# Layer 1's gate: root and inverse lengths placed half a step earlier in the order of work

## The reference

```python
qkv = shift_token(x) @ wqkv               # 8 heads of 64
q = l2norm(q) * q_scale                   # t / max(|t|, 1e-12)
k = l2norm(k) * k_scale
q, k = rotary_xpos(q, k)
o = local_attention(q * 8, k, v)          # windows of 64, each sees itself and the one before
x = x + o @ wo
h = layernorm(shift_token(x)) * lg + lb
a, g = split(h @ w1 + b1)
x = x + (a * gelu(g)) @ w2 + b2
```

## Time and profile before

| | us |
|---|---|
| median of 3 runs (5014.09 to 5020.99) | 5015.04 |
| the profiled execution | 5018.97 |
| its span | 5017.2 |
| mean granted clock of PE | 0.948 |
| PE, DVE, ACT, POOL busy in the span | 4451.9, 3169.0, 2488.4, 2285.9 |

### The profile page before, as it was taken

One profiled execution on the slowest core, in us unless ns is written; L12 is line 12 of the kernel. 1 busy time (PEld: TensorE's weight loads), 2 busy tenths in 40 slices (PEclk: granted clock), 3 DMA queues, 4 the chain that ended last, 5 costly groups with the idle time before them and its releaser, 6 DMA issues. The chain is left out here.

```text
span 5017.2 us, 68570 instructions
## 1 busy us (share of the span) xinstructions
PE 4451.9 (89%) x27252; PEld 2196.7 (44%) x27252; DVE 3169.0 (63%) x4190; ACT 2488.4 (50%) x3838; POOL 2285.9 (46%) x1307
## 2 busy tenths in 40 slices
PE   6999999997886788887789999996799999999998
PEld 3444444444564334333322222222455555555554
DVE  4756575736665777773278777865565666666565
ACT  2344444446664466562256666663344444444444
POOL 0455555567773487790100000000166666676674
PEclk8999999998998799898889999997899999999999
DMA  1000000002110000000000000000000000000000
GB/s 33 3 3 3 3 3 3 3 1 59 31 31 19 3 2 1 2 1 24 3 1 1 2 2 1 1 1 16 5 1 3 3 1 3 3 3 1 3 1 9
DMA packets 62001, 36.80 MB, mean 7 GB/s; under 512 B 36356, under 2 KB 53936, under 8 KB 61424
## 3 DMA queue, kind: packets, MB, share of 16 engines
q1 hardware_dynamic: 61680, 32.41, 2.5%
HBM read 22.03 MB, written 1.05 MB: 5 GB/s over the span
## 5 line engine op out<-in xcount | busy, mean ns | idle before, releaser
L799 DVE TENSOR_REDUCE L_part<-banks 128x2 f32<-128x1024 f32 (+2 forms) x1600 | 1880.4, 1188 | 938.7 <-PE banks L650 810.3
L784 ACT ACTIVATE L_weights<-banks 128x1024 f32<-128x1024 f32 (+1 forms) x1600 | 1556.4, 999 | 1063.7 <-PE banks L682 836.3
L708 PE MATMUL banks<-L_weights,L_V 128*32 128x512 f32 (+3 forms) x6400 | 1491.4, 603 | 2.8 <-ACT L_raw L733 1.8
L1035 POOL TENSOR_TENSOR L_wsum<-L_wsum,L_weights 128x1024 f32<-128x1024 f32 (+3 forms) x436 | 962.1, 2207 | 54.1 <-ACT L_weights L784 2.4
L1018 POOL TENSOR_TENSOR L_wsum<-L_wsum,L_two 128x1024 f32<-128x1024 f32 x238 | 568.0, 2386 | 823.3 <-DVE L_two L1000 820.5
L708 PEld LDWEIGHTS banks<-L_weights,L_V 128*64 128x64 f32 (+1 forms) x6400 | 282.7, 123 | 467.8 <-issue 406.0
L2433 POOL MEMSET A3m_ones<- 128x128 f32 x1 | 0.2, 204 | 1060.2 <-POOLq L97 1060.2
L650 PE MATMUL banks<-L_KH,L_QH 64*128 64x512 f32 (+3 forms) x1664 | 399.6, 437 | 45.4 <-DVE L_part L799 27.5
L682 PE MATMUL banks<-L_QH,L_KH 64*128 64x512 f32 (+3 forms) x1664 | 410.3, 428 | 18.1 <-issue 10.2
L682 PE MATMUL banks<-L_QL,L_KH 64*128 64x512 f32 (+3 forms) x1664 | 371.7, 382 | 0.0
L682 PE MATMUL banks<-L_QM,L_onesrow 64*128 64x512 f32 (+3 forms) x1664 | 371.6, 381 | 0.0
(11 more groups left out here) (438 smaller groups left out, 5873.3 us busy)
## 6 DMA issues: line engine op xcount, KB each, us to landing
F_early<-F_V SPq DMA_DIRECT2D x63, 128.0 KB, 2.3
F_tab<-xpos SPq DMA_DIRECT2D x8, 512.0 KB, 4.2
F_h<-L_ffn_h_w SPq DMA_DIRECT2D x2, 1024.0 KB, 8.2
F_wqkv<-L_ffn_wqkv SPq DMA_DIRECT2D x2, 768.0 KB
L_cos<-rope_cos SPq DMA_DIRECT2D x1, 1024.0 KB, 5.6
L_sin<-rope_sin SPq DMA_DIRECT2D x1, 1024.0 KB, 7.7
out<-X SPq DMA_DIRECT2D x4, 256.0 KB, 2.3
F_z<-F_x SPq DMA_DIRECT2D x32, 31.8 KB
```

Of the source, the lines that this page charges most:

```text
L708: mm = pe.e.matmul(O[r, c:BANK], self.V[g % 2][:, kt, h, :], self.W[x % self.NW][:, y, c:BANK], start=kt < starts, stop=kt >= tiles - starts)
L784: act.e.activation(self.W[x % self.NW][:, :, c:BANK], self.banks(it)[:, :, c:BANK], ACT.Exp, scale=self.scale).then_inc(self.exped, 1)
L799: dve.e.tensor_reduce(self.part[n % 3][:, pr, j, p, :], self.banks(it)[:, :, 0:wide], AX.X, ALU.max).then_inc(self.mx_read, 1)
L1035: pool.e.tensor_tensor(acc[:, :, c:BANK], acc[:, :, c:BANK], W[:, :, c:BANK], ALU.add).then_inc(self.summed, 1)
```

## The change

The items root and lengths of each unit are put one half step earlier. Their code, ranks, waits and signals stay as they are. In the list, root(u) now closes half step 8u-8, behind the exponentials' first half, the spin of (0, queries) and the V product of tile 1, and lengths(u) stands in half step 8u-7, behind the score, statistics and moments of unit u-2 and ahead of unit u+1's first products. Between root and the norm of unit u-2 now stand the second half of a tile's exponentials and the two squares of unit u+1.

```diff
@@ TransformerGate.plan
             put(first - 9, ("table", u))
-            put(first - 7, ("root", u))
-            put(first - 6, ("lengths", u))
+            put(first - 8, ("root", u))
+            put(first - 7, ("lengths", u))
             for r, i, x in self.SPINS:
                 put(first + r, ("spin", u, i, x))
```

## The result

The changed kernel takes **5028.9 us** (median of 18 runs, 5023.2 to 5033.1) against 5014.1 us for the kernel before on the same chip (18 runs): a ratio of 1.0028, 95% interval 1.0022 to 1.0034, so 14.8 us slower. Forecast were 5020, a range of 5000 to 5034, and "within 0.2%" as the likeliest case; 0.28% is slower. In the profiled executions the gate of layer 1 ends 14.4 us later, 1.0 us of which is its later start, and what follows it is 3.0 us shorter.

What follows compares the result with a forecast made beforehand. The prediction took layer 1's gate to be bound by PE waiting for GpSimd's first keys, themselves waiting for the lengths. Terms -4.2 + 4.0 + 5 x 1.0 gave +4.8 us, from 5015.04 to about 5020, range 5000 to 5034.

Steps and rivals of the forecast that it cites:

- the sum: Whole change: start -4.2, unit 2 +4.0, units 3 to 7 5 x 1.0, giving +4.8 us.
- the case held likeliest: Whole change: the earlier keys' gain is given back, -6 to +13 us, 5009 to 5028; chance 0.60.
- the first wait: PE's 45.5 us wait in layer 1's gate for GpSimd's first keys, expected to nearly go.
- the lock's size: VectorE's small layer norm operations wait out GpSimd's instructions: 7.4 us instead of 2.47, 4.9 more per layer norm.
- net +1.0 us per unit: Units 3 to 7: the 4.1 us gained by earlier keys is more than given back, +1.0 each.
- what stands behind the stall: Unit 4, layer norm's end to third GELU: 1368.0 to 1378.0, with oT at 1372.7 after the statistics.
- Up to 0.8 more per unit: PE's half clock behind a 5.3 us stall for the z transposes: up to 0.8 us more per unit.
- The start: Unit 0: root after the V copy, keys' spin at 1165.4 instead of 1168.40, a 1.19 us wait gone: -4.2 us.
- Unit 2's lengths: Four of seven operations wait beside GpSimd's query spins, about 3.1 us; with the layer norm, third GELU about +4.0 us.
- Slower: the lock reaches the lengths in every unit: VectorE's seven lengths operations in step 8u-7 wait 3.1 us in five more units: +15.5, 5035; chance 0.17.
- faster: Small layer norm operations slip between GpSimd's instructions: 4986 with no wait, 5002 with half; chance 0.20.

Runs made afterwards that it cites:

- experiment 8: Changed kernel with GpSimd spinning each unit's first keys before the kT copy, without waiting for unit u-2's layer norm: 5019.0 us against 5016.0 before.
- experiment 11: Kernel before, with GpSimd squaring an unread scratch tile four times behind the kT copy in units 1 to 6: 5025.4 us against 5011.2.
- experiment 5: Changed kernel plus six unread PE products in units 0 to 5, before the z transposes' bank is taken: 5028.4 us, ratio 1.0029.
- keys first: Changed kernel with GpSimd spinning a unit's first keys before the kT copy, then waiting for unit u-2's layer norm: 4993.0 us against 5016.0 before.

## Where the prediction was right, and where it was wrong

The time lies in the range, 9 us above the 5020 that the sum gave, and outside the case held likeliest. The way there was as forecast, with one term of the sum much too small.

**Right: the first wait goes, a second takes its place.** The keys' wait went, PE's wait moved to the z transposes (5.79 us in unit 4; 5.3 forecast), half clock behind it, 12 loads of 1.28 us. What ends that wait is the join's add (L2017) behind the layer norm, which frees the bank, and not L2108 itself. The ov copy made oT 2.6 us late by unit 4's own anchor (forecast 2.4). The Trainium skill's rule ("ScalarE: Activation LUTs", What ACT_TABLE_LOAD costs) of 2.66 us a switch has no support here: in the changed kernel the root starts at 1354.26, 0.02 us behind a load of 1.28 us that began at 1352.96, 0.01 us behind the V copy, and with the root alone the 12 added loads cost 12.7 us in all, 1.1 us each.

**Right, partly by luck: the lock's size.** 4.9 us per layer norm were forecast, and the groups give 4.9. How it is made up was not as forecast: L2104, put at 1.3 us, slipped into a gap at 1367.36 and took 0.17, and the four L2108, put at 1.8 us together (0.7 for the first one's wait and 1.1), took 3.73. Two errors cancelled. The prediction said that no row showed whether L2104 waits; it does, when it meets an instruction: 1.19 us in experiment 8, 0.90 in experiment 11. The Trainium skill ("SBUF — State Buffer", Who interferes with whom) has a VectorE operation in a two-port mode, which a `tensor_scalar` such as L2104 can enter, and a GpSimd operation exclude each other for a whole instruction; the rows agree.

**Wrong: the step "net +1.0 us per unit".** It measured 2.8. In the profiled executions the last unit's third GELU comes 14.7 us later, 9.9 more than the sum of 4.8: the five units are 8.9 of that and the gate's later start is 1.0; what is left nearly cancels. In unit 4 (2.6 us) the layer norm ended 0.3 us later than put, by the third GELU of the unit before (4.1 us late), and from there unit 4's third GELU came 11.3 us later (1372.43 to 1383.71) where the prediction had 10.0 (1368.0 to 1378.0). That is the mis-sized term: **what stands behind the stall**. The prediction let oT wait for z's transfer alone and put it 4.7 us behind the layer norm's end; it came 5.9 us behind. The statistics were in time (4.0 us, 3.9 forecast); oT then waited 1.04 us for PE's values, at half clock. From oT to the third GELU it was 5.4 us, 5.3 forecast. "Up to 0.8 more per unit" for the clock was close to this 1.0, but kept out of the sum. And the clock would have been the wrong remedy, since the prediction also took all small VectorE operations behind the layer norm at their undisturbed durations: L2025 took 1.08 us and L2073 0.99. With the clock restored (experiment 5) oT does come 4.8 us behind, but the wide copy then waits for a GpSimd instruction, and the time stays. What a kernel without either would take is open; no run here takes away both.

**The start** gave 3.1 us (the transposes of unit 1's keys, 1215.37 to 1213.30, in a stage that began 0.99 us later), 4.2 forecast. Unit 2's lengths took 4.3 us, less than the 5.4 that its term held; unit 1's were long too (5.1, before 4.1), where the prediction had unit 2 only. Together these two terms come to +0.5 net of the later start, -0.2 forecast: no matter.

**The cases.** "Slower: the lock reaches the lengths in every unit" did not happen: in units 3 to 7 they took 2.3 us, as without a lock; in unit 4 GpSimd was idle for 16 us around them. The case "faster" fell, as the small operations don't slip through. Without any lock the prediction put the change at 4986; no run takes the lock away from the changed kernel's own order, but keys first, where four of the six layer norms are free of it, gives 4993. The likeliest case's range ended at 5028, one microsecond under the result, but its chances were put on "within 0.2%": a sum of +4.8 with a known cost of up to 0.8 a unit outside it should have stood at +9, with about even chances of slower.

## What to carry to other kernels

- Before releasing an engine earlier, look at what it will run beside. Here GpSimd's idle time was what kept VectorE's chain of small operations fast: a release 4 us sooner cost 5 us of waiting on VectorE, and one wait added at the right place was worth 28 us.
- The wait in the profile named GpSimd's keys and the lengths, but the gain lay in the order of GpSimd's queue, once the lengths were early: first the work that VectorE's results allow, then a pause for VectorE's small chained operations, then the rest.
- Two costs that hide behind one another don't add: halves of this change cost 12.7 and 12.8, the whole 14.8. Terms that are each worked out with the others absent need not add up to the whole.

## What was not expected of the hardware

- Four VectorE operations in a row (L2108, 0.28 us each alone) took 3.73 us together beside GpSimd and 1.11 to 1.12 with GpSimd idle: the engine that has just run doesn't keep its turn. In experiment 8 it was 2.77 us.
- Chained operations alternate: one ends with the GpSimd instruction that it met, the next may slip through the 0.08 to 0.1 us between two instructions (L2104 at 1367.36, L2103 at 1362.31 in experiment 11). Which ones depends on where they meet: in the changed kernel L2103 and L2105 took 1.1 to 1.2 us, in experiment 8 L2104.
- The wide copy, one input of 128x512 elements, shows it too: 0.43 us alone, 1.46 beside GpSimd, while the operations that read PSUM (L2002, L2059, L2063, L1986) kept 0.69, 0.68, 0.68 and 1.22 us throughout.
